# Early-fusion transformer on one core: engine orders of two mixers, first groups of two stages, later clearing of semaphores

## The reference

```
h = concat(patches @ W + b, text_block(tokens))            # 32 x 114 x 256
h = h + delta_net(layernorm(h))   # conv(4)+silu of q,k,v; per head and token:
    S = S*exp(g); S = S + k (beta*(v - S k)); o = S q       # then o*silu(z), rms norm, W_out
h = h + moe(layernorm(h))         # 32 experts, top 4, capacity 256, and a shared expert
h = h + state_mixer(layernorm(h)) # conv+silu, softplus steps, per sample:
    y = (sum_l x_l * delta_l B_l / L) . C + D*x ; y*silu(z) @ W_out
h = h + factorised_mlp(layernorm(h))                       # entmax gates, two low-rank layers
```

## Time and profile before

| what | value |
|---|---|
| median of 3 runs | 2904.06 us (2903.47 to 2907.8) |
| the profiled execution's own time | 2906.16 us |
| its span | 2904.1 us |
| TensorE, VectorE, ScalarE, GpSimd busy | 83%, 69%, 44%, 29% |
| granted TensorE clock, mean | 0.901 |
| mixer, from its first to its last instruction | 745.2 to 1993.5 us |
| route | 1997.6 to 2223.0 us |
| state mixer | 2335.0 to 2699.0 us |

### The profile page before, as it was taken

How to read it: one execution, slowest core, us unless ns; L and a number is a source line. 1 busy time by engine, 2 the same in 40 slices (tenths; PEclk the granted TensorE clock), 3 DMA queues, 4 the chain that set the end, 5 groups by cost and what they waited for, 6 DMA issues and landing times. The chain is left out here.

```text
span 2904.1 us, 53774 instructions
## 1 busy us (share of the span) xinstructions
PE 2398.6 (83%) x19286; PEld 1822.4 (63%) x19286; DVE 2005.7 (69%) x4812; ACT 1292.0 (44%) x3118; POOL 827.9 (29%) x708
## 2 busy tenths in 40 slices
PE   7999998996559998898999899875552937889698
PEld 6777766885437777676767667664342825666454
DVE  4888883334488998898889889743661446886673
ACT  1444442121457776676767677631000314344132
POOL 2111100001133333333333333322774066350110
PEclk9999998996679999999999999987666967899799
DMA  4211001003112222121212122211213932110000
GB/s 150 93 52 29 14 6 55 22 25 124 58 40 52 58 55 52 48 55 48 54 49 56 47 53 57 53 47 62 62 30 109 293 101 59 35 53 1 21 25 26
DMA packets 274342, 168.97 MB, mean 58 GB/s; under 512 B 182847, under 2 KB 250318, under 8 KB 273728
## 3 DMA queue, kind: packets, MB, share of 16 engines
q1 hardware_dynamic: 247949, 140.28, 17.0%
q0 software_dynamic: 26112, 25.03, 3.3%
HBM read 99.23 MB, written 73.45 MB: 59 GB/s over the span
## 5 line engine op out<-in xcount | busy, mean ns | idle before, releaser
L1289 POOL TENSOR_TENSOR qd<-decay,qm 114x456 f32<-114x456 f32 x128 | 142.6, 1128 | 515.8 <-DVE qm L1405 509.8
L1799 PE MATMUL d_ps<-d_xT,w_qkv 128*128 128x228 f32 x1024 | 217.5, 362 | 13.6 <-DMA d_xT<-normed_t 13.6
L1799 PEld LDWEIGHTS d_ps<-d_xT,w_qkv 128*128 128x128 f32 x1024 | 197.0, 195 | 39.4 <-issue 15.6
L1386 DVE TENSOR_TENSOR ue<-ue,elim_tmp 128x30 f32<-128x30 f32 (+14 forms) x480 | 206.4, 430 | 16.7
L1566 ACT ACTIVATE decay<-d_ps,gates 114x114 f32<-114x114 f32 x512 | 139.9, 357 | 142.3 <-PE d_ps L1787 83.7
L1384 DVE TENSOR_TENSOR elim_tmp<-ue 128x30 f32<-128x30 f32 (+14 forms) x480 | 185.7, 387 | 25.0 <-issue 10.1
L2504 POOL DMA_INDIRECT s_eo<-rows_y,slots_all x128 | 152.4, 1191 | 148.6 <-POOLq L87 110.6
L1448 DVE SCALAR_TENSOR_TENSOR y_v<-raw,taps,y_v 128x228 f32<-128x228 f32 x384 | 158.9, 487 | 42.0 <-ACT y_v L1604 42.0
L1448 DVE SCALAR_TENSOR_TENSOR y_qk<-raw,taps,y_qk 128x228 f32<-128x228 f32 x384 | 146.5, 450 | 25.3 <-ACT y_qk L1604 25.3
L2095 POOL DMA_INDIRECT rows_x<-r_xn,slot x128 | 144.4, 1128 | 51.6 <-issue 50.0
L1577 ACT ACTIVATE gl<-upto,gates 114x114 f32<-114x114 f32 x512 | 156.1, 393 | 1.2 <-PE d_ps L1787 0.8
(11 more groups left out here) (343 smaller groups left out, 5578.5 us busy)
## 6 DMA issues: line engine op xcount, KB each, us to landing
rows_x<-zero_row SPq DMA_DIRECT2D x4, 2048.0 KB
ue<-blocks_n SPq DMA_DIRECT2D x16, 512.0 KB, 4.9
blocks_u<-ue SPq DMA_DIRECT2D x16, 512.0 KB, 2.7
blocks_v<-on SPq DMA_DIRECT2D x16, 512.0 KB, 2.9
e_x<-rows_x SPq DMA_DIRECT2D x32, 256.0 KB, 4.3
e_gu<-L_ffn_w_gate_up SPq DMA_DIRECT2D x32, 256.0 KB, 4.1
rows_y<-e_y SPq DMA_DIRECT2D x32, 256.0 KB, 3.2
blocks_n<-nt SPq DMA_DIRECT2D x96, 64.0 KB
```

What stands on the lines that cost most here:

```text
L1289: pool.tensor_tensor(qd[p.par][s][:, hs(u), :].rearrange("p (a o b) t -> p a o b t", o=2, b=2)[:, :, o], e[o][:, :, :].rearrange("p (a b) ...
L1386: step = dve.tensor_tensor(ue[:, 0:j, j + 1:], ue[:, 0:j, j + 1:], part, ALU.subtract)
L1799: last = pe.matmul(ps[:, f % 2, (t % 2) * W:(t % 2 + 1) * W], w_qkv[:, k, t * 128:(t + 1) * 128], xT[:, k, :], start=(k == 0), stop=(k == ...
```

## The change

Four things are changed.

1. **Semaphores.** The clearing block is gone. A stage's semaphores are cleared in the next stage by SyncE, behind its first loads (`c.clear_old(sp)`); the last stage's in a block of their own at the end.
2. **Mixer.** The hand-written orders of VectorE, ScalarE, GpSimd and TensorE in `iteration` are replaced. The instructions are the same ones. The weights `w_qkv`, `w_z` and `w_out` now lie in the tile that later holds `c.resid`; behind the last projection SyncE loads the first 3 groups of `c.resid` (`early_rows`).
3. **Route.** The first group's order: `choose(0)`, `place(0)` come ahead of statistics of group 2, weights and the shared expert; the counts on TensorE come ahead of the shared expert's products, and TensorE first waits for the gate's weights alone. GpSimd puts the third power behind 4 scatters. In all groups `place` comes ahead of `share` and `shared`.
4. **State mixer.** The first two groups' rows are gathered with a semaphore per sample and added sample by sample; powers stand behind fewer gathers; the orders of VectorE, ScalarE and TensorE in a group are replaced.

```
     def stage(self, build, *args):
-        with ExitStack() as names:
-            self.sem_ctx, self.sems = names, []
-            build(self, *args)
-            used = self.sems
-            with self.nc.Block() as block:
-                @block.sync
-                def _(sp):
-                    for s in used:
-                        sp.sem_clear(s)
+        names = ExitStack()
+        self.sem_ctx, self.sems = names, []
+        build(self, *args)
+        self.old_ctx.close()
+        self.old_ctx, self.old = names, self.sems
+    def clear_old(self, sp):
+        for s in self.old:
+            sp.sem_clear(s)
...
+                def early_rows():
+                    sp.wait_ge(qkv_mm, PAIRS * 8)
+                    for g in range(EARLY):
+                        sp.dma_start(c.resid[:, g * GS + 1:(g + 1) * GS + 1, :],
+                                     hid[g * GS:(g + 1) * GS].rearrange("b s d -> s b d")).then_inc(r_in, 16)
...
                 statistics(1)
-                for g in range(GROUPS):
+                normalise(1)
+                choose(0)
+                place(0)
+                statistics(2)
+                share(0)
+                shared(0)
+                add_shared(0)
+                for g in range(1, GROUPS):
...
                 gather(0, 0, GS)
                 pool.memset(raw[:, :, :, 0:TAPS - 1], 0.0).then_inc(s_init, 1)
-                gather(1, 0, GS // 2)
+                gather(1, 0, 1)
                 power(0)
-                gather(1, GS // 2, GS)
-                gather(2, 0, GS)
+                gather(1, 1, GS)
+                gather(2, 0, 2)
                 power(1)
...
                 for n in range(4, G):
+                    if n + 1 < G:
+                        gather(n + 1, 0, GS // 2)
                     power(n)
...
-                add_first()
-                norm(0)
+                add_first(0, range(GS))
+                norm_stats(0)
+                norm_scale(0)
+                add_first(1, range(2))
...
-                silu_z(0)
-                silu_y(0)
-                add_routed(1)
+                for t in range(CT):
+                    silu_z(0, t)
+                for t in range(CT):
+                    silu_y(0, t)
+                add_first(1, range(2, GS))
+                norm_stats(1)
+                norm_scale(1)
                 step_sizes(0)
-                norm(1)
```

More of the change, by code:

```diff
@@ L1115, in need, with __init__, shift, sample @@
         eng.wait_ge(sem, count)
+class Pair:
+    def __init__(self, j, off):
+        self.j, self.off = j, off
+        self.n = j * 2 + off
+        self.par = off % 2
+    def shift(self, d):
+        return Pair(self.j, self.off + d)
+    def sample(self, s):
+        return self.n * 2 + s
+def need(eng, sem, count):
+    if not isinstance(count, int) or count > 0:
+        eng.wait_ge(sem, count)
 def delta_net(c, hid, xts):
@@ L1536, in iteration @@
                     if proj:
+                        silu(nxt, 0)
+                    if z:
+                        gated(r, 1)
+                    if proj:
                         silu(nxt, 1)
                     if z:
-                        gated(r, 1)
                         gated(r, 2)
@@ L2089, in power, with scatter @@
                     pool.tensor_tensor(rstd[:, :], rstd[:, :], c.minus_half[0:S, 0:GS], ALU.pow).then_inc(rrstd, 1)
-                def scatter(g):
+                def scatter(g, samples):
                     pool.wait_ge(slot_r, g + 1)
-                    for s in range(GS):
+                    for s in samples:
                         for k in range(TOPK):
@@ L2101, in _ @@
                 pool.wait_ge(c.zeros_out, 16 * (SLOTS // 2048))
-                for g in range(GROUPS):
+                scatter(0, range(1))
+                power(2)
+                scatter(0, range(1, GS))
+                for g in range(1, GROUPS):
                     if g + 2 < GROUPS:
                         power(g + 2)
-                    scatter(g)
+                    scatter(g, range(GS))
                 for p in range(3):
@@ L2280, in _ @@
                 turn(0)
+                pe.wait_ge(rg_in, 16)
                 gate_logits(0)
+                turn(1)
+                counts(0)
+                pe.wait_ge(rw_in, 32)
                 gate_up(0)
-                for g in range(GROUPS):
+                gate_logits(1)
+                down(0)
+                gate_up(1)
+                for g in range(1, GROUPS):
                     if g + 1 < GROUPS:
@@ L2480, in state_mixer @@
         s_eo = [c.gpsimd_dma_sem(f"s_eo_in{k}") for k in range(EO)]
-        s_first = [c.gpsimd_dma_sem(f"s_eo_first{k}") for k in range(GS)]
+        s_first = [c.gpsimd_dma_sem(f"s_eo_first{k}") for k in range(2 * GS)]
         SW = 6
@@ L2643, in _ @@
                         add_routed(n)
-                    if j + 1 < G:
+                    if more:
+                        step_sizes(j + 1)
+                    for n in ahead[:1]:
+                        norm_stats(n)
+                    result(j)
+                    for n in ahead[:1]:
+                        norm_scale(n)
+                    if more:
                         step_gates(j + 1)
-                    for n in ahead[:1]:
-                        norm(n)
-                    result(j)
                     for n in ahead[1:]:
                         add_routed(n)
-                        norm(n)
+                        norm_stats(n)
+                        norm_scale(n)
                 ch.sync()
@@ L2687, in tanh_z, with token_read @@
                     act.activation(sz[j % 2][:, t, :], ps[:, t, 0:L], ACT.Tanh, scale=0.5).then_inc(sthz, 1)
-                def token_read(j):
-                    if j:
+                def token_read(j, first, last):
+                    if j and first == 0:
                         act.wait_ge(y_mm, 4 * j)
-                    for s in range(GS):
+                    for s in range(first, last):
                         act.wait_ge(xt_mm, 4 * j + s + 1)
@@ L2845, in _ @@
                         state_inputs(j + 1)
+                    early = j >= len(AHEAD)
+                    if early and j + 2 < G:
+                        turn(j + 2)
                     project_out(j)
                     if j + 2 < G:
-                        turn(j + 2)
+                        if not early:
+                            turn(j + 2)
                         project_x(j + 2)
```

377 lines of the change are left out of this document (211 added, 166 removed).

## The result

The changed kernel takes 2869.76 us (median of 4 runs, 2865.57 to 2876.15) against 2903.76 us of the kernel before on the same chip. The ratio is 0.9885, with a 95% interval of 0.9866 to 0.9904: 34 us faster, where 47 were forecast. The profiled executions took 2866.58 and 2906.16 us, 39.6 us apart.

| stage | before | after | moved | forecast |
|---|---|---|---|---|
| seven gaps | 15.8 | 0.1 | -15.7 | -15.5 |
| mixer | 1248.3 | 1265.6 | +17.3 | -8 |
| route | 225.4 | 215.5 | -9.9 | -10.3 |
| state mixer | 364.1 | 333.3 | -30.8 | -17.3 |
| the other five | 1047.7 | 1047.6 | -0.1 | +4 |

A forecast was written before the change was run, and what follows sets the result against it. Four limits: idle gaps, VectorE's stretch in mixer rounds, route's start-up, state mixer's gathers. Terms -15.5, -10.3, -9.8, -7.5, -8 gave -51, less 4 given back: -47, 2857 us against the median; likeliest range 2840 to 2875, rivals 2822 to 2892.

The forecast's parts named there:

- likeliest case: Whole kernel: all parts sum to -47 us, 2857 us against the median; own range 2840 to 2875, chance 0.52.
- first stretch: Mixer round, from VectorE's first elimination step to the end of the copy turning the inverse: about 38 us, before 36.1.
- Semaphores and route: Gaps between stages go, -15.5 us; route's statistics, logits and first scatter start earlier, -10.3 us.
- ten plain rounds, four heads: Mixer loop: plain rounds' first stretch 2.3 us longer, heads' waits go (-1.2), gated fills waits (-0.6 each): sum +10.
- choice of -8: Mixer: -8 us taken between the +10 sum and -26; bounds -36 and +34.
- count of stalls: Mixer: VectorE steps laid beside GpSimd's instructions lose 5.7 us a round against 4.7 before; the mixer's sum is +10.
- favourable case: Mixer: second `gate_scale` meets PSUM readers, memset misses the mean; 2.6 us more a round, mixer -26; hidden-stalls rival, chance 0.25.
- The five losses of the prediction: Mixer's first stretch: VectorE loses 0.75, 0.75, 0.8, 1.8 and 1.5 us beside GpSimd's instructions, given as 5.7 us.
- 1.5 us for each of some five groups: State mixer's later groups: earlier gathers and TensorE's earlier turn shorten waits, -7.5 us; bounds 0 and -14.
- The mixer's rounds get longer: Rival, mixer: stalls fall as laid, at loop heads too; +2.4 us on 14 rounds, +34, total 2899; chance 0.11.
- Slower: Rival, mixer: ScalarE's delayed work reaches past the join, 5.2 us on each of 14 rounds, total 2934; chance 0.05.
- The first groups don't start earlier: Rival, route and state mixer: early loads not done or count and gathers still wait; -27 missing, 2884; chance 0.07.

## Why the prediction was right, and where it was not

The time of 2870 us lies within the likeliest case's own range of 2840 to 2875, near its slow end, and the signs that were named for this case came: gaps of 0.1 us, a first stretch of 37.4 us (about 38), a step of 2.03 us beside the second `gate_scale`. But that the sum came out so near is in part luck, since the mixer's term and that of the state mixer's later groups were wrong in opposite directions.

*Semaphores and route* came out within half a microsecond of their terms, and their runs alone confirm them: 14 us measured for the first, 7.8 us for the early loads (7.0 in the sum).

*Mixer: the step that failed is "ten plain rounds, four heads", and with it the choice of -8.* The sum counted loop rounds and left out the turns in which a table of orders runs with parts switched off. The filling turns cost 13.0 us in this pair of profiles, some 10 in the others, of the 25.3 by which the term was wrong. The rest is choice: the count of stalls gave +10, and I then moved to -8, between that and the favourable case. Rounds and tail came out at +4.3, nearer to the count, though two profiles of one order differ by as much. Plain rounds came out at +1.4 us in the first stretch (2.3 forecast), heads at -2.3 (-1.2). The second `gate_scale`, the memset on the mean's small instruction and the `query_decay` pairs fell where they had been laid. Whole rounds followed: +1.25 us for each of ten, -2.5 for each of four heads, which nearly balance. (The five losses of the prediction add up to 5.6 us, not to 5.7.)

*State mixer: the mis-sized term is "1.5 us for each of some five groups".* The start came out well: 11.3 us at the second convolution for 9.8. A later group gave 5.8 us, and all behind the second convolution 19.5 us instead of 7.5, more than the bound of 14. I had read two waits of one group, 3.67 and 1.01 us, and priced them; the measure that was needed is one row, TensorE's busy time and clock over a group, which shows 3.9 us idle and a clock of 0.92. The clock had no place in the sum. Which of the stage's new orders gave how much stays open, beyond the 7 us of TensorE's turn.

*Rivals.* "The mixer's rounds get longer" (+34 in the mixer) named the direction, not the place. The recorded range ended at 2892 us, below that rival's own 2899. "Slower" asked for 3.1 us a round and ScalarE behind the join: the round grew by 0.2. "The first groups don't start earlier" is refuted by the rows. That stages give 4 us back did not show: the other five stages sum to the same.

## What to carry to other kernels

An order that is tuned for the full turn of a software pipeline also runs in the turns that fill it: price these apart, from their own waits. Where stalls are moved, ask for each engine what it waits for once they are gone: VectorE's stretch shrank by 1.8 us and the round by nothing; with TensorE's input moved as well, plain rounds shrank and heads grew by more. And where TensorE is the bound of a loop, one window over a turn (busy, clock) says what its waits are worth, since closing them also gives back the clock.

## What the runs showed of the hardware

- A GpSimd power of 114x16 on SBUF for 3 us stretches nothing beside it; a product of 114x1024 stretches the one two-input VectorE step that meets it to its own end (2.03 us for 0.29), and a step that reads PSUM not at all. With a memset in the product's place the step took 0.29 us.
- Beside the memset of 1282.72 VectorE's small TENSOR_SCALAR took 0.87 us (0.17 elsewhere) and the half behind it 0.78 (0.41), both to the memset's end; beside the memset that follows the second `gate_scale` the halves kept their time. The whole trace of the changed kernel says the same: in 14 rounds this TENSOR_SCALAR, which reads one tile, met a memset, and each time it took 0.86 to 0.87 us and the half behind it 0.78; of 48 halves that met a memset without it, all but one kept their 0.4 us or less.
- TensorE's clock fell inside otherwise full loops, and the products behind the hole took 1.6 to 1.7 times as long: behind a wait of 3.34 us 3.29 us for 1.97, behind 3.56 us 6.40 for 3.83 and behind 4.06 us 1.90 for 1.17.
- The last stage, which no kernel here touches, took 201 us in the profiled executions of four kernels and 207 us in those of ten, with nothing in its instructions changed. So the parts were read from stage lengths, and not from differences of times alone. TensorE's granted clock goes with it: in the third 25 us of the stage it was 0.93 in each of the four and 0.73 in each of the ten, between 150 and 175 us 1.00 against 0.93. What sets the clock there was not tried.
